# Token tiles split before they are transposed, and transposed by a DMA instead of TensorE, in a mixture-of-experts stage

## The reference

```
h = layernorm(x) * (1 + cb) + sb
expert_idx = argmax(h @ Wr.T + br)                   # one of 8
hid = relu(h @ W1[expert].T + b1[expert])            # 256 -> 1024
y   = hid @ W2[expert].T + b2[expert]                # 1024 -> 256
x   = x + gb * y
```

## Time and profile before

| what | value |
|---|---|
| median of 3 runs | 525.43 us (524.94 to 526.74) |
| profiled execution | 522.24 us, its span 519.7 us |
| mean granted TensorE clock | 0.948 of full speed |
| PE busy | 459.2 us (88%) |
| PE weight loads (PEld) busy | 405.7 us (78%) |
| DVE busy | 398.2 us (77%) |
| ACT busy | 326.3 us (63%) |
| POOL busy | 303.8 us (58%) |

### The profile page before, as it was taken

One profiled execution on the slowest core, in us unless ns is written; L12 is line 12 of the kernel. 1 busy time (PEld: TensorE's weight loads), 2 busy tenths in 40 slices (PEclk: granted clock), 3 DMA queues, 4 the chain that ended last, 5 costly groups with the idle time before them and its releaser, 6 DMA issues.

```text
span 519.7 us, 15163 instructions
## 1 busy us (share of the span) xinstructions
PE 459.2 (88%) x4392; PEld 405.7 (78%) x4393; DVE 398.2 (77%) x1054; ACT 326.3 (63%) x863; POOL 303.8 (58%) x463
## 2 busy tenths in 40 slices
PE   4899999999999999995127999999999999999980
PEld 3688888888888888884116989888898888888970
DVE  2679998888889899886873777777777777777750
ACT  2437777766676777764025776777677766777650
POOL 2337777777777777656142466657665765566531
PEclk9989999999999999997556999999999999999996
DMA  8654444333334463111002112211221122111000
GB/s 287 249 190 146 141 140 122 125 122 123 120 138 131 142 216 103 69 42 41 11 6 77 33 55 74 64 53 56 72 67 58 46 66 67 55 53 50 22 13 0
DMA packets 23968, 47.37 MB, mean 91 GB/s; under 512 B 4719, under 2 KB 17650, under 8 KB 21752
## 3 DMA queue, kind: packets, MB, share of 16 engines
q1 hardware_dynamic: 17976, 32.74, 18.9%
q0 software_dynamic: 4992, 12.60, 7.8%
q10 hardware_dynamic: 960, 1.57, 0.9%
HBM read 36.14 MB, written 13.51 MB: 96 GB/s over the span
## 4 chain that ended last, share of the span: by engine, by line
PE 40%; issue 23%; POOL 22%; DVE 8%; POOLq 3%; DMA 1%; ACT 0%; ACTq 0%; DVEq 0%
PE ps_qk L1076 10%; POOL arena L488 9%; POOL out_rows L496 9%; PE ps_va L1082 5%; PE ps_o L1028 5%; PE ps_kv L1036 5%; POOL arena L476 4%; PE ps_va L1064 3%; PE ps_o L1024 3%; POOLq L483 2%; PE ps_h L1091 2%; PE ps_h L1043 2%; PE ps_k L1051 2%; PE ps_x L1100 1%; DMA w<-in_wmod 1%
## 5 line engine op out<-in xcount | busy, mean ns | idle before, releaser
L1164 PE MATMUL ps_o<-w,arena 128*128 x936 | 108.7, 273 | 2.9 <-DVE arena L988 1.6
L1164 PEld LDWEIGHTS ps_o<-w,arena 128*128 128x128 f16 x936 | 89.3, 98 | 17.4 <-issue 6.9
L958 DVE COPY w<-w 128x2048 f16 x78 | 59.4, 761 | 31.3 <-issue 21.1
L597 ACT ACTIVATE arena<-ps_qk,arena 128x128 f32<-128x128 f32 x156 | 44.5, 368 | 59.5 <-PE ps_qk L1144 59.4
L476 POOL TENSOR_TENSOR arena<-arena 128x256 f32<-128x256 f32 x39 | 28.1, 722 | 67.5 <-DVE arena L992 67.5
L1076 PE MATMUL ps_qk<-arena,wqkv_sb 128*128 128x128 f32 x512 | 65.0, 282 | 0.0
L1144 PE MATMUL ps_qk<-arena,w 128*128 128x128 f16 x936 | 60.1, 222 | 4.2 <-DVE arena L975 3.4
L1144 PEld LDWEIGHTS ps_qk<-arena,w 128*128 128x128 f16 x936 | 54.1, 99 | 11.6 <-issue 7.2
L1076 PEld LDWEIGHTS ps_qk<-arena,wqkv_sb 128*128 128x128 f32 x512 | 62.3, 199 | 0.9 <-DMA bqk_sb<-in_bqk 0.9
L1144 PE MATMUL ps_va<-arena,w 128*128 128x128 f16 x936 | 59.9, 221 | 0.0
L488 POOL DMA_INDIRECT arena<-token_rows,slot_token x39 | 51.3, 1315 | 12.9 <-issue 12.9
(11 more groups left out here) (163 smaller groups left out, 925.3 us busy)
## 6 DMA issues: line engine op xcount, KB each, us to landing
w<-in_w_raw SPq DMA_DIRECT2D x16, 1024.0 KB, 5.3
token_rows<-arena SPq DMA_DIRECT2D x64, 128.0 KB, 1.9
arena<-in_x SPq DMA_DIRECT2D x32, 128.0 KB, 2.1
b_sb<-in_b2b SPq DMA_DIRECT2D x1, 1024.0 KB, 6.7
w<-in_wmod ACTq DMA_DIRECT2D x1, 768.0 KB, 9.3
wqkv_sb<-in_wqkv SPq DMA_DIRECT2D x1, 768.0 KB, 8.6
mod_rows_sb<-mod_rows SPq DMA_DIRECT2D x1, 768.0 KB, 5.2
arena<-token_rows,slot_token POOLq DMA_INDIRECT x39, 3.7
```

Of the source, the lines that this page charges most:

```text
L597: last = act.activation(hid[:, f, :], bank[("qk", "va")[h]][:, (f % 4) * P:(f % 4 + 1) * P], ACT.Relu, bias=consts_now[:, r, f:f + 1], sca ...
L958: dve.tensor_copy(now[:, :, i * F // 2:(i + 1) * F // 2], of[:, :, i * F // 2:(i + 1) * F // 2]).then_inc(s_w1, 1)
L1164: last = pe.matmul(bank["o"][:, 0:D], hid_parts[:, r % 2, b, f, :], w[:, bass.ds(m + 1, 1), a, f * D:(f + 1) * D].rearrange("p a d -> p (a ...
```

## The change

Before, a gathered tile of float32 rows was transposed on PE, and ACT and DVE split the transposed result, read from PSUM, into the two fp16 parts. Now ACT and DVE split the rows as they were gathered, token by token, into `tok16` (two buffers, 128 tokens x 512 fp16), and one `dma_start_transpose` per tile on SP's queue writes the four transposed 128x128 blocks into `tok_parts`, which has four buffers now. ACT and DVE do this for the tile two ahead (lag -2) where they did it for the tile one ahead (lag -1), at the same places of their slots. The waits follow the data: ACT now waits for the gather itself, PE's first layer for the transposing DMA.

```diff
-        tok_s = cut(2, DK * P)
+        tok_s = cut(4, DK * P)
+        tok16 = cut(2, D).bitcast(F16)
...
+            for n in range(NT):                                    # SP
+                g, r = divmod(n, 4)
+                sp.wait_ge(s_tlo, n + 1)
+                need(sp, s_hp, 2 * (n - 3))
+                sp.dma_start_transpose(tok_parts[:, r].rearrange("p i k t -> p (i k) t"),
+                                       tok16[:, r % 2]).then_inc(s_tt[r], 16)
...
-                if it := ffn_item(k, u, -1):                       # ACT
+                if it := ffn_item(k, u, -2):
                     n, g, r = it
-                    act.wait_ge(s_tx, n + 1)
-                    need(act, s_hp, 2 * (n - 1))
-                    act.activation(tok_parts[:, r % 2, 0], bank["h"][:, 0:D].rearrange("p (k t) -> p k t", k=DK),
-                                   ACT.Copy, scale=x_scale).then_inc(s_thi, 1)
+                    act.wait_ge(s_in[r], 16 * (g + 1))
+                    need(act, s_tt[(r + 2) % 4], 16 * (g + r // 2))
+                    act.activation(tok16[:, r % 2, 0:D], tok[:, r, D:2 * D], ACT.Copy, scale=x_scale).then_inc(s_thi, 1)
...
-                                                                   # DVE
+                if it := ffn_item(k, u, -2):
                     n, g, r = it
                     dve.wait_ge(s_thi, n + 1)
-                    dve.scalar_tensor_tensor(tok_parts[:, r % 2, 1],
-                                             bank["h"][:, 0:D].rearrange("p (k t) -> p k t", k=DK), x_scale,
-                                             tok_parts[:, r % 2, 0], ALU.mult, ALU.subtract).then_inc(s_tlo, 1)
+                    dve.scalar_tensor_tensor(tok16[:, r % 2, D:2 * D], tok[:, r, D:2 * D], x_scale,
+                                             tok16[:, r % 2, 0:D], ALU.mult, ALU.subtract).then_inc(s_tlo, 1)
...
-                    pe.wait_ge(s_tlo, n + 1)                       # PE, first layer of tile n
+                    pe.wait_ge(s_tt[r], 16 * (g + 1))
...
-                if it := ffn_item(k, u, -1):                       # PE, transposes of the tile ahead
-                    n, g, r = it
-                    pe.wait_ge(s_in[r], 16 * (g + 1))
-                    need(pe, s_tlo, n)
-                    for h in range(DK):
-                        last = pe.transpose(bank["h"][:, h * P:(h + 1) * P],
-                                            tok[:, r, D + h * P:D + (h + 1) * P], ident)
-                    last.then_inc(s_tx, 1)
```

More of the change, by code:

```diff
@@ L159, in build @@
         tile_matrix = sb("tile_matrix", [P, NT], I32)
-        arena = sb("arena", [P, 9216])
+        arena = sb("arena", [P, 9280])
         at = [0]
@@ L168, in cut @@
             at[0] += n
-            assert at[0] <= 9216, at
+            assert at[0] <= 9280, at
             if len(shape) == 2:
@@ L203, in build @@
         gate_part = cut(2, D)
-        tok_s = cut(2, DK * P)
+        tok_s = cut(4, DK * P)
+        tok16 = cut(2, D).bitcast(F16)
         hid_s = cut(2, FK * P)
         consts_now = cut(4, FK + 2)
-        assert at[0] <= 9216
+        assert at[0] <= 9280
         tile_consts = sb("tile_consts", [P, NE, FK + 2])
@@ L283, in build @@
         s_in = [sem(f"tokens_gathered_{r}") for r in range(4)]
+        s_tt = [sem(f"tokens_transposed_{r}") for r in range(4)]
         s_out = [sem(f"rows_scattered_{r}") for r in range(4)]
-        (s_idx, s_prep, s_tx, s_tt, s_hp, s_ha, s_hd, s_hx, s_hta, s_htd, s_y, s_ys, s_done) = map(sem, (
-            "tokens_cleared", "tile_constants_step", "tokens_transposed", "tok_t_ready",
+        (s_idx, s_prep, s_hp, s_ha, s_hd, s_hx, s_hta, s_htd, s_y, s_ys, s_done) = map(sem, (
+            "tokens_cleared", "tile_constants_step",
             "hidden_done", "hidden_ready_act", "hidden_ready_dve", "hidden_transposed", "hid_t_ready_act",
             "hid_t_ready_dve", "y_done", "y_step", "rows_done"))
-        scratch = arena[:, 4 * 2 * D:9216]
+        scratch = arena[:, 4 * 2 * D:9280]
         chosen16 = scratch[:, 384:512].bitcast(F16)
@@ L1144, in slot @@
                                     last = pe.matmul(bank[name][:, (f % 4) * P:(f % 4 + 1) * P],
-                                                     w1_now[:, a, at_w:at_w + P], tok_parts[:, r % 2, b, h, :],
+                                                     w1_now[:, a, at_w:at_w + P], tok_parts[:, r, b, h, :],
                                                      start=(q == 0 and h == 0), stop=(q == 2 and h == DK - 1))
                         last.then_inc(s_hp, 1)
-                if it := ffn_item(k, u, -1):
-                    n, g, r = it
-                    pe.wait_ge(s_in[r], 16 * (g + 1))
-                    need(pe, s_tlo, n)
-                    for h in range(DK):
-                        last = pe.transpose(bank["h"][:, h * P:(h + 1) * P],
-                                            tok[:, r, D + h * P:D + (h + 1) * P], ident)
-                    last.then_inc(s_tx, 1)
                 if it := ffn_item(k, u, 1):
```

## The result

The changed kernel takes 663.3 us (median of 4 runs, 661.27 to 664.38) against 525.29 us before (4 runs): ratio 1.2616, 95% interval 1.2587 to 1.2646. Forecast were 671 us and a range of 635 to 715. The profiled execution took 661.27 us, its span is 659.5 us, 139.8 more than before.

What follows compares the result with a forecast made beforehand. PE, DVE and ACT were read as all close to their limit. Profiled 522.24 + 141 (ring) + 1.4 (start) - 0.9 (end) = 663.7, as a median 666.9, plus 4 for the clock: 671 us, range 635 to 715.

Steps and rivals of the forecast that it cites:

- The ring: Expert stage: each gather waits, through ACT, DVE and POOL, for the previous gather's landing; 651 to 683 us, chance 0.58.
- The landing: From a gather's issue on POOL to its data being there: 3.7 us at the median, plus 0.1 until ACT notices.
- ACT's wait: Sign named in advance: ACT's split of the tokens waits for the gather's DMA about 4 us in each of 35 slots.
- The turn: One slot of the expert stage: terms summing to 9.84 us against 5.81 before, 4.03 more.
- 35 turns: Gathers of tiles 4 to 38 wait for a finished tile, the first four do not: 35 x 4.03 = 141 us.
- The transposing DMA: One per tile on SP's queue, taken to land after 3.7 us (1.9 to 9.3), hidden in the steady state.
- The start: Before tile 0's first layer the transposing DMA is not hidden: first layer at 279.1 instead of 276.03, about 1.4 us remaining.
- the end: After the last turn PE is two us further ahead: -0.9 us.
- the estimate of 5.2 us for four: Four 128x128 blocks transposed by DMA at the skill's 1309 ns each: an estimated 5.2 us, hidden as well.
- The clock: PE pauses 4.1 us per turn and falls from 2.4 to 1.2 GHz: 0.1 us per turn, 4 us added.
- the low clock as a bound: Rival: PE's clock stays at 1.2 GHz and PE bounds the slot at 10.45 us: 688 us, chance 0.10.
- a quicker gather with idle engines: Rival: the gather lands in 2.7 us with engines idle around it, turn 8.84 us: 632 us, chance 0.11.

Runs made afterwards that it cites:

- e2: The kernel before, with PE's transposes and the split on ACT and DVE moved to the tile two ahead, no transposing DMA: 786.8 us, ratio 1.498.
- e4: The changed kernel with the tokens' split, still for the tile two ahead, placed last in the slots of ACT and DVE: 541.1 us, ratio 1.027.
- e5: The changed kernel with the gather in two, the normed rows gathered four tiles ahead and first in POOL's slot: 517.04 us, ratio 0.9932.
- e12: The changed kernel with eight buffers, one whole gather per tile, four tiles ahead and before POOL's wait for DVE: 506.28 us, ratio 0.9730.
- e3: The changed kernel with one idle POOL operation of 128x256 floats added between the residual's sum and the next gather: 677.6 us, ratio 1.289.
- e7: The changed kernel with two transposing DMAs per tile, one after the other, the first into an unused buffer: 663.9 us, ratio 1.276.
- e1: The changed kernel with the split on ACT and DVE for the tile one ahead instead of two: 622.8 us, ratio 1.185.

## Why the prediction was right

- **The ring** stood as named: ACT waits for the gather in each slot, and the waits behind it are those listed. `e2` (early use, no DMA transpose), `e4` (same use, nothing behind it), `e5` and `e12` (earlier issue) each show its closing or opening, and `e3` that POOL is on it. The landing, 3.96 us in the turn shown, cost nothing before and now stands in every turn; the Trainium skill's rule to issue a DMA early and wait for it late ("DMA: Bandwidth & Descriptors", rules for kernel authors) agrees. ACT's wait was 5.5 us and not about 4: I had read 4.3 off the old slot, but ACT has only 4.3 us of work in a turn of 9.8.
- **The turn**: 9.84 us summed, 9.81 measured. In the turn shown the parts are 1.77 (1.77), 3.96 (3.7 and 0.1), 2.19 (2.18) and 2.20 (2.09); over all turns they are 1.78, 3.71, 2.20 and 2.13. That the two totals agree to 0.03 is partly luck: the 31 turns of 9.96 us are 0.12 longer than the sum, and the four with quick landings, of which the sum knew nothing, bring the mean back by 0.15.
- **35 turns**: 140.1 us measured, 141 summed. Counting 35 and not 39, because the first four gathers are free, mattered; four turns more would have made it 16 us longer (4 x 4.03). The last three slots, with no gather to wait for, took 5.02, 4.71 and 4.41 us.
- **The transposing DMA**: I took 3.7 us between 1.9 and 9.3, its median was 2.4. The error was free in the turns, as said (`e7`). At the start it was no error: the first one was issued at 274.12 and PE went on at 278.38, 4.3 us later.
```profile
269.21 1.26 POOL L497 DMA_INDIRECT arena<-token_rows,slot_token  x1 [0.77 <-issue]
...
272.91 0.51 ACT L634 ACTIVATE arena<-arena,small 128x256 f16<-128x256 f32 x1 [10.92 <-DMA arena<-token_rows,slot_token]
...
278.38 2.72 PE L1151 MATMUL ps_qk<-arena,w 128*128 128x128 f16 x24 [12.13 <-DMA arena<-arena]
```
The first layer of tile 0 still came earlier than the 279.1 summed, since the first gather was issued 0.95 us earlier than before (270.16). The start cost 0.9 us instead of 1.4, the end gave back 1.2 instead of 0.9. The Trainium skill ("VectorE: DVE Perf Modes", the three transpose paths) prices one block; the estimate of 5.2 us for four made from it in the prediction is twice the 2.4 us measured, and the measurement decides.

- **The clock** is the term that was mis-sized. It fell, to 0.88 in the window shown, and I added 4 us for it; the turns show no such cost. In 12 turns the second half of the first layer took 1.50 us and in 21 it took 2.3 to 2.7; less their landings these turns are 6.08 and 6.11 us at the mean. PE waited for ACT's ReLU, 96.9 us in 36 slots or 2.7 us each, so its stretched work ended inside the turn (in the turn shown it paused 3.4 us there and 0.9 before the second layer, not 4.1 in one). The clock also stretched PE's busy share, 67% in the window shown where I had named 57%. Without the clock's term the sum was 666.9 for a measured 663.3. Of these 3.6 us, 1.2 are the distance from the profiled execution to the median, which I took over from before as 3.2 and which was 2.0.
- **Not tested**: the low clock as a bound did not occur, and a quicker gather with idle engines did not either: outside the four short turns the landing was 3.84 us at the mean, with ACT's start in it, against 3.8 summed.
- **What I would not have got right** are the experiments' sums. In `e2` I left the second layer out of the ring though it stood in line behind the waiting transposes; the prediction asked that question for ACT only, since there PE does not wait.

## What to carry to other kernels

Before moving a use ahead, read how long before it the data are issued, and follow what stands behind the new wait in every engine's written order: if the issue itself is among it, the landing time of a DMA enters every turn of the loop. Moving work off the engine that is busy 98% gained nothing while another engine's sequence set the slot; together with a gather that had its lead and its buffers it was part of a kernel 2.7% faster (the kernel before with eight buffers and its own transposes was not tried). In these kernels a falling clock cost time only where the slowed engine was in the ring.

## What the runs showed of the hardware

- The transposing DMA of 128 x 512 fp16 values within the core's memory took 1.19 us of issue on SP's queue and landed after 2.4 us, 0.5 us more than a plain store of the same 128 KB. In `e1` its longest landing was 5.9 us, and in `e5`, which issues one more DMA per slot, the median of 26 was 3.1.
- A DVE operation with two inputs in memory beside a POOL operation with two inputs took 1.25 us at the mean instead of 0.48:
```profile
L985 DVE SCALAR_TENSOR_TENSOR arena<-mod_rows_sb,slot_late,arena 128x256 f32<-128x256 f32 x34 | 42.4, 1248 | 0.0
```
This is `e5`, where POOL's third issue had moved its L497 beside it. In `e12` the same operation took 0.48 us again. In `e3`, where the added POOL operation stood beside it, both grew in the turn read: DVE's to 0.94 us, and POOL's to 1.17, where its residual's sum of the same shape took 0.72.
